# A graph transformer layer on one core: TensorE's loop over token groups written out, and a reordered last group

## The reference

```
nx = layernorm(x); q, k, v = nx @ Wq + bq, nx @ Wk + bk, nx @ Wv + bv
scores = q k^T / 8, where adj is false: -1e9; attn = softmax(scores)
x = x + (attn v) @ Wo + bo
nx = layernorm(x)
out = x + gelu(nx @ W1 + b1) @ W2 + b2        # 512 -> 2048 -> 512
```

## Time and profile before

| what | value |
|---|---|
| median of 3 runs | 2171.91 us (2171.76 to 2173.87) |
| profiled execution | 2175.16 us, span 2173.0 us |
| PE (matmul) | 2127.1 us busy, 98% of the span |
| DVE, ACT, POOL | 69%, 42%, 20% of the span |
| mean granted TensorE clock | 0.994 |

### The profile page before, as it was taken

How to read it: one execution, slowest core, us unless ns; L and a number is a source line. 1 busy time by engine, 2 the same in 40 slices (tenths; PEclk the granted TensorE clock), 3 DMA queues, 4 the chain that set the end, 5 groups by cost and what they waited for, 6 DMA issues and landing times.

```text
span 2173.0 us, 33121 instructions
## 1 busy us (share of the span) xinstructions
PE 2127.1 (98%) x13200; PEld 1759.6 (81%) x13200; DVE 1496.1 (69%) x2227; ACT 903.3 (42%) x1321; POOL 429.8 (20%) x293
## 2 busy tenths in 40 slices
PE   8998999999999998999999999999999999999999
PEld 6787878787878887788888888888888888888887
DVE  7886778688988985666666666666666666666433
ACT  4443434343333444345345345345345345345332
POOL 1332333331111115103103103103103103103200
PEclk9999999999999999999999999999999999999999
DMA  5343434432212114444544544534534534534532
GB/s 185 118 144 126 142 128 137 133 127 65 65 65 65 45 50 175 185 155 176 212 154 174 214 151 175 215 149 177 216 147 178 216 146 179 217 144 180 218 122 96
DMA packets 103840, 323.96 MB, mean 149 GB/s; under 512 B 21408, under 2 KB 29600, under 8 KB 87328
## 3 DMA queue, kind: packets, MB, share of 16 engines
q1 hardware_dynamic: 98192, 321.68, 40.6%
q10 hardware_dynamic: 5520, 0.55, 0.2%
HBM read 265.57 MB, written 56.62 MB: 148 GB/s over the span
## 4 chain that ended last, share of the span: by engine, by line
PE 93%; DVE 3%; issue 2%; POOL 1%; ACT 1%; DMA 0%; SPq 0%; ACTq 0%; DVEq 0%; POOLq 0%
PE lin L182 10%; PE lin L183 9%; PE lin L184 9%; PE ps_r L182 5%; PE ps_x L182 5%; PE ps_r L184 5%; PE ps_r L183 5%; PE ps_x L184 5%; PE ps_x L183 5%; PE ps_out L184 5%; PE ps_out L182 5%; PE ps_out L183 5%; PE ps_z L182 3%; PE ps_z L184 3%; PE ps_z L183 3%
## 5 line engine op out<-in xcount | busy, mean ns | idle before, releaser
L1214 DVE TENSOR_TENSOR acc<-ps_r,acc 128x512 f32<-128x512 f32 x256 | 176.7, 690 | 328.4 <-PE ps_r L184 327.6
L826 ACT ACTIVATE snaps<-ps_x 128x512 f32<-128x512 f32 x192 | 114.6, 597 | 411.0 <-PE ps_x L184 410.8
L182 PE MATMUL ps_r<-w_ring,h_ring 128*128 128x512 f32 x512 | 199.4, 389 | 1.6 <-DVE h_ring L1204 1.6
L182 PE MATMUL ps_x<-nxc,w_ring 128*128 128x512 f32 x512 | 199.9, 390 | 0.0
L184 PE MATMUL ps_x<-nxc,w_ring 128*128 128x512 f32 x512 | 199.7, 390 | 0.0
L183 PE MATMUL ps_x<-nxc,w_ring 128*128 128x512 f32 x512 | 199.7, 390 | 0.0
L184 PE MATMUL ps_r<-w_ring,h_ring 128*128 128x512 f32 x512 | 199.2, 389 | 0.0
L182 PE MATMUL ps_out<-w_ring,h_ring 128*128 128x512 f32 x512 | 199.2, 389 | 0.0
L184 PE MATMUL ps_out<-w_ring,h_ring 128*128 128x512 f32 x512 | 199.2, 389 | 0.0
L183 PE MATMUL ps_r<-w_ring,h_ring 128*128 128x512 f32 x512 | 199.2, 389 | 0.0
L183 PE MATMUL ps_out<-w_ring,h_ring 128*128 128x512 f32 x512 | 199.2, 389 | 0.0
(11 more groups left out here) (134 smaller groups left out, 5061.4 us busy)
## 6 DMA issues: line engine op xcount, KB each, us to landing
w_ring<-w_scratch SPq DMA_DIRECT2D x64, 1792.0 KB, 7.3
w_ring<-w_scratch SPq DMA_DIRECT2D x64, 1024.0 KB, 7.1
xb<-x_scratch SPq DMA_DIRECT2D x22, 1024.0 KB, 9.7
xres<-in_x SPq DMA_DIRECT2D x64, 256.0 KB, 2.7
x_scratch<-xres SPq DMA_DIRECT2D x64, 256.0 KB, 2.2
x<-in_x SPq DMA_DIRECT2D x15, 1024.0 KB, 7.7
acc<-x_scratch SPq DMA_DIRECT2D x32, 256.0 KB, 2.8
out<-xb SPq DMA_DIRECT2D x32, 256.0 KB, 2.0
```

Of the source, the lines that this page charges most:

```text
L182: pe.matmul(out, lhs[1], rhs[0], start=first, stop=False, skip_group_check=resumed)
L826: act.activation(snaps[:, j], ps_x[:, :], ACT.Copy).then_inc(snap_done[j], 1)
L1214: dve.tensor_tensor(acc(t), ps_r[:, :], acc(t), ALU.add).then_inc(acc_added, 1)
```

## The change

On TensorE the loop over groups 1 to 12 is replaced by straight code: groups 1 to 15 are each written out, with constants in their waits (and so without the extra semaphore steps). In group 15, POOL adds the bias to tile (14, 3) and fills the buffer for pair (15, 1) before the four `conv_lo`; the wait for `shifted` ahead of `conv_lo(1)` goes, and the wait for `prob_done` of pair (15, 0) moves from ahead of `conv_lo(2)` to ahead of `conv_lo(1)`. ACT copies the transposes of pair (15, 0) before the exponential of pair (15, 1), not after it.

```
@@ POOL, last_body(g) @@
                 fill_neg(g, 0)
                 t_sum(0, 2)
                 t_sum(0, 3)
+                bias_xres(g - 1, 3)
+                fill_neg(g, 1)
                 conv_lo(0)
-                bias_xres(g - 1, 3)
-                pool.wait_ge(shifted, PAIRS * g + 1)
+                pool.wait_ge(prob_done, PAIRS * g + 1)
                 conv_lo(1)
-                fill_neg(g, 1)
-                pool.wait_ge(prob_done, PAIRS * g + 1)
                 conv_lo(2)
                 pool.wait_ge(shifted, PAIRS * g + 2)
                 conv_lo(3)
@@ ACT, last_body(g) @@
                 exponent(g, 0)
+                take_probT(g, 0)
                 exponent(g, 1)
-                take_probT(g, 0)
                 att_hi(g, 0)
@@ TensorE @@
             body(-1, 1)
             body(0, 0)
-            with pe.Fori(1, NG - 4, 2) as g:
-                body(g, 1)
-                body(g + 1, 0)
-            for g in range(NG - 3, NG):
+            for g in range(1, NG):
                 body(g, g % 2)
```

## The result

| what | before | after |
|---|---|---|
| median | 2172.77 us (2171.76 to 2173.87, 4 runs) | 2138.28 us (2136.95 to 2139.41, 4 runs) |
| ratio | | 0.9841 (95% interval 0.9824 to 0.9858) |
| profiled execution, span | 2175.16, 2173.0 us | 2137.51, 2135.4 us |

The change saves 34.5 us of the median; the forecast was 2136.1, from 2132.5 to 2142.

A forecast was written before the change was run, and what follows sets the result against it. The prediction took PE to bound the kernel, idle or slowed at the attention loop's taken branches. Its terms, 31.6 + 2.6 + 0 + 1.6 = 35.8 us, taken from 2171.91 gave 2136.1 us, range 2132.5 to 2142.

The forecast's parts named there:

- Part 1: Attention loop's five taken branches on TensorE: 31.6 us saved, 22.6 of it idle time and 9.0 the low clock behind it.
- part 2: Twelve attention groups, 0.22 us leaner each without register work and extra semaphore steps: 2.6 us saved, bounds 0 and 3.
- rival 2: Groups behind the branches: another engine becomes the bound without the pauses, 1 us in each of five groups, 2141 us; chance 0.05.
- Part 3: Straight code's instruction fetch at dense spots of small matmuls: no cost, 0 us; upper bound 4.16 us at one spot.
- rival 3: Straight code arrives late at some dense spots: three stalls with low clock behind each cost 18 us, 2154 us; chance 0.06.
- rival 4: Code arrives late at nearly all 24 dense spots of groups 1 to 12: slower than before, 2279 us at full price; chance 0.03.
- rival 5: Gaps belong to something else at the start of odd groups, only parts 2 and 4 act: 2167.7 us; chance 0.01.
- Part 4: Last group's reordering: O0 3 us and F1 1.0 us earlier, plus 0.6 us of clock: 1.6 us saved, bounds -1.5 and 5.0.
- main case: Whole kernel, the forecast's own case: 2136.1 us, from 2132.7 to 2138; chance 0.70.
- rival 1: Last group: low part 0 ahead of DVE's scaling delays residual and SP's weights; -1.5 to 0 us, say 2138.5; chance 0.15.

The follow-up runs named there:

- e1: Kernel before with only POOL's and ACT's reordering in group 15, the loop over groups 1 to 12 kept: 2173.82 us, ratio 1.0002 to the kernel before.
- e2: Kernel before with groups 1 to 15 written straight and group 15 in its old order, run twice: 2137.91 us and 2139.21 us.
- e4: Changed kernel with TensorE's MLP loop over super groups 1 to 6 written out too: 2140.25 us, ratio 0.9850 to the kernel before.
- e3: Changed kernel with three extra semaphore steps ahead of each product and down projection in TensorE's MLP loop: 2143.49 us, ratio 0.9861 to the kernel before.
- e5: Attention loop over groups 1 to 12 back, its pass cut to an MLP pass's length by leaving out low-part products: 2102.78 us, with less work.
- e10: Changed kernel with a two-group TensorE loop back, as long as the old one but cut between U4 and U5, behind long matmuls: 2141.34 us, ratio 0.9849.
- e0: The changed kernel again, unaltered, as yardstick for the runs on its chip: 2138.62 us, ratio 0.9837 to the kernel before.
- e8: Changed kernel with F1's weights loaded before group 15's tiles and DVE taking value tile 1 before pair (15, 1): 2134.26 us, ratio 0.9817.
- e9: Changed kernel with F1's weights and value tile 1 early, and POOL's group 15 work placed between DVE's two-input instructions: 2133.55 us, ratio 0.9814.
- e6: Changed kernel with the loop's extra semaphore steps behind the waits of scores and attention outputs kept in straight code: 2139.29 us, one run.

## Why the prediction was right

**Part 1 (five back edges, 31.6 us) and part 2 (leaner groups, 2.6 us)** came to 34.2 us; groups 1 to 13 measured 683.62 - 648.21 = 35.4 us shorter. Of the surplus of 1.2 us, 0.65 is group 1, which lasts 49.88 us, not 50.75: it was 0.63 us longer than other loop groups, 0.3 of it a wait for DVE's tile of attention outputs that is gone now. The straight groups average 49.86 us, where 49.90 was counted, which gives most of the rest. No other wait took the branch's place: rival 2 is out. DVE's 46.1 us fit into 49.88. e1 and e2 split the change: all that can be measured is in the straight code.

**Part 3 (code arrives in time)** holds: no "issue" wait in 15 straight groups, and none in e4 with a much longer stream. Rivals 3, 4 and 5 are out.

**The mechanism** named under part 3 is shown from both sides (a pass's length is the count of TensorE's instructions in the trace from one branch to the next, e3's that plus the 360 added): e5 shortens the pass from 1911 to 1527 and the branch falls from 4.2 to 0.2 us; e3 lengthens an MLP pass from 1527 to 1887 and it rises from 0.2 to 3.5 us. The fetches say the same: one block in five passes of e5, 44 in those of e3. Where between 1527 and 1887 instructions the limit lies was not tried. This fits what the Trainium skill states on TensorE's 2048 instructions ("Runtime: NRT & Kernel Launch", Instruction fetch mechanics), if blocks fetched ahead count too, which no run here shows, and contradicts the same section's sentence on two blocks. What the forecast did not see is the second condition, shown by e10 and e3: the fetch at the branch costs PE only what the queued matmuls don't cover. The old loop was cut behind 128 matmuls that PE passes in 2.2 us.

**Part 4 (last group, 1.6 us)** was right step by step and most likely wrong in its sum. Forecast and measured: scaling 2.9 and 2.87 us; O0 3 and 2.88 us earlier; F1 1.0 and 1.0 us earlier, on the landing of its weights. But e1 has no gain (ratio 1.0002), and the pair e2, e0 has 0.6 us with overlapping ranges. 1.6 us lies at the very edge of e1's interval, so it is unlikely and not excluded. The mis-sized term is the clock: 0.6 us of it was counted as won, and the 1.0 us of F1 as passing through. PE still idles 5 us in two pieces ahead of F1, and the clock falls as before. Where the low stretch ends (P1 at g14 + 69.2 or 69.9 in two profiles of one kernel, 69.3 or 70.5 in two of e2) moves the result by as much as the whole edit. When the waits of O0 and F1 both go (e8), F1 and F5 run at full clock; its profile has a low stretch only behind P1's wait, and in e9, without that wait, there is none.

**The total was helped a little by luck.** Parts 1 to 3 gave 1.2 us more than counted, part 4 up to 1.6 us less, and two errors of opposite sign leave a saving of 34.5 us against the 35.8 forecast; what is left between the parts and the total lies within the spread of the medians. The time misses by 2.2 us, not 1.3, because the median of before rose from 2171.91 to 2172.77 with one more execution. Among the forecast's own cases, 2138.28 us lies just above the main case's upper end of 2138 and next to rival 1's 2138.5: that rival had the right size of outcome, but not its cause, since F1 did start earlier.

## What to carry to other kernels

Read the branch instructions' own durations and the windows on either side of them. In these runs a taken branch lasted 3.3 to 6.1 us when TensorE's pass was 1887 or 1911 instructions long, and 0.2 us at 1527. It hurts only where PE has no long matmuls queued. Write such a loop out, shorten its pass, or at least cut it behind long matmuls. In a chain with several waits in a row, a step that moves forward by 3 us can come out as nothing in the time: here the next wait took 2 us of it, and the low clock behind the idle time could take the rest.

## What the runs showed that was not expected

- A branch of 3.3 to 3.6 us can be wholly hidden: in e10 no idle time of PE at four of them.
- A loop group is 0.2 to 0.4 us longer than a straight one, while two to four plain semaphore steps cost at most 0.04 us (e6). That the rest is the register work ahead of the waits is what is left over, not shown.
- The length of the low clock's stretch differs between executions of one kernel (6.8 and 10.2 us in two profiles of the changed kernel), enough to hide an edit worth 1 us. The windows of that stretch, in the profile above and in e0, show a mean granted clock of 0.50, that is 1.2 GHz, behind the same two idle pieces:

```profile
806.76:813.59 6.83, 4.74 (x61) 3.88 (x52) 4.30 (x5) 1.44 (x2) 3.69 (x3) 0.50 1.00 424
```

```profile
805.80:816.00 10.20, 7.90 (x79) 6.47 (x80) 5.31 (x7) 4.76 (x6) 4.72 (x3) 0.50 0.99 421
```
